# A two-layer perceiver kernel: keys and values projected in other pieces around the transposes, and a weight rounding spread over steps and engines

## The chip, the cores and the metric

One core of one Trainium2 chip. The metric is the device time of one launch in microseconds (us); lower is better. All times of single instructions come from one profiled execution.

## The reference

Two layers, each of a cross attention over 1,024 context positions, a self attention and a gated feed-forward, with a layer norm ahead of each part. Batch 16, 64 latents of width 256, 16 heads of 16. What matters here:

```
x = x + _L0_xattn(ctx, ctx, layernorm(x), mask, ...)   # softmax(q k^T / 4 + mask * -1e9) v, then Wo
x = x + _L0_attn(layernorm(x), ...)
x = x + _L0_ffn(layernorm(x), ...)    # weights rounded to int8 steps: round(w / scale) with scale = max|row| / 127
x = x + _L1_xattn(layernorm(x), ctx, ctx, ...)         # softmax(q k^T / 4) v, then Wo; no mask
x = x + _L1_attn(layernorm(x), ...)
x = x + _L1_ffn(layernorm(x), ...)    # weights and activations rounded to fp4 in blocks of 16
```

## The kernel before

Each engine has its own program, an order written out by hand; semaphores join them. Both cross attentions run as a loop of `STEPS` = 64 steps `s` (16 batches of 4 groups of heads). The first is `first_layer`, the second is in `second_layer`, where the self attention and the start of the feed-forward of finished tiles are woven into the same steps: `tile_at(s, lag)` names the tile whose piece of work stands at step 10 + lag + 8 t.

One step of a cross attention, engine by engine. **TensorE (PE):** `scores` (L801, L807) puts the scores into banks 2 and 3 with queries on partitions and into banks 0 and 1 with keys on partitions; `transposes(s - 1)` (L830) turns the probabilities of the step before, in two halves with a bank each; `project_v(s + 2)` (L755) makes values, one bank, two parts; `turn_column_max` (L814) turns the vector of column maxima; `spread_top` (L821) spreads their overall maximum; `project_k(s + 4)` (L739) makes keys, one bank, two accumulating parts; in even steps `times_v` (L847 to L860, bank "pv") multiplies with the values. **VectorE (DVE):** `column_maxima` (L979; masked L971 and L976), `row_maxima` (L991; masked L988), `tops` (L998), which needs `turn_column_max`, and `below_tops` (L1014 and L1016; masked L1009), which needs `spread_top`. **ScalarE (ACT):** `take_t` (L936), `exponentials` (L919), which needs the row maxima, `take_v` (L909), `take_k` (L882), `column_exponentials` (L927). **GpSimd (POOL):** sums of columns (`spread_rows` L712, `add_columns` L697 to L703), mask conversion, joining of heads. In the second layer `scores(s + 1)` wait for `below_tops(s)` and `exponentials(s)`; in the first for the two maxima of step s alone.

The banks that everything except the scores and the two maxima's transposes uses are a ring of three (5, 6, 7), given out by `Banks.open` in the order in which PE's program opens them. An opening waits until the last holder of that bank has been read out (`taken`), and PE runs in order:

```
        if bank is None:
            bank = self.rotating[self.turn % len(self.rotating)]
            self.turn += 1
        wait(pe, self.taken[bank], self.count[bank])
```

In the second layer only 9 of 16 batches project keys in the loop (steps 4 to 11, 16 to 27, 32 to 43, 56 to 59); the keys of `EarlyKeys.BATCHES` are made earlier and loaded.

The weights of the feed-forwards are made ready inside these loops. `Int8Weights` (first layer; three matrices x, starting at `IW_STEPS` 4, 16, 28) does five steps on DVE: maxima, scale, inverse, rounding of all pieces (L450), subtraction of the rounding constant with conversion to bf16 for all pieces (L457); then three bank units "i" are transposed by PE and taken by ACT. `Fp4Weights` (second layer) does eight DVE steps at `FW_AT`, one on POOL at `FW_SCALE`, and three units "w" at `FW_TRANSPOSE`.

Of the kernel before, what the change touches and what calls it, by code (L numbers as in the profile page):

```python
# [18 lines left out]
ALU = mybir.AluOpType  # L19
# [11 lines left out]
FF = 704  # L31
# [360 lines left out]
class Int8Weights:  # L392
# [3 lines left out]
    STEPS = 5  # L396
# [31 lines left out]
    def step_on_vector(self, dve, x, n):  # L428

        pieces, width = (IC, D) if x < 2 else (KD, FF)  # L430
        first = x * IC
        scale = self.scale[:, first:first + pieces]
        raw = self.raw[:, 0:pieces * width].rearrange("p (c n) -> p c n", n=width)
        whole = self.whole[:, 0:pieces * width].rearrange("p (c n) -> p c n", n=width)
        if n == 0:
            if x == 0:
                dve.wait_ge(self.pad_set, 1)
            dve.wait_ge(self.loaded, (32, 64, 80)[x])
            dve.tensor_reduce(self.mag[:, 0:pieces], raw, AX.X, ALU.max, apply_absolute_value=True)\
                .then_inc(self.step, 1)  # L440
        elif n == 1:
            dve.wait_ge(self.step, 3 * x + 1)
            dve.tensor_scalar(scale, self.mag[:, 0:pieces], 1.0 / QMAX, None, ALU.mult).then_inc(self.step, 1)
        elif n == 2:
            dve.wait_ge(self.step, 3 * x + 2)
            dve.reciprocal(self.inv[:, 0:pieces], scale).then_inc(self.step, 1)
        elif n == 3:
            dve.wait_ge(self.step, 3 * x + 3)
            for c in range(pieces):
                dve.tensor_scalar(raw[:, c, :], raw[:, c, :], self.inv[:, c:c + 1], ROUND, ALU.mult, ALU.add)\  # L450
                    .then_inc(self.rounded, 1)
        else:
            if x >= 1:
                self.banks.wait_filled(dve, ("i", x - 1, self.UNITS - 1))
            for c in range(pieces):
                dve.wait_ge(self.rounded, first + c + 1)
                dve.tensor_scalar(whole[:, c, :], raw[:, c, :], ROUND, None, ALU.subtract).then_inc(self.ready, 1)  # L457
# [119 lines left out]
class CrossAttention:  # L577
# [246 lines left out]
    def transposes(self, pe, s):  # L824

        pe.wait_ge(self.exp_done, s + 1)
        for h in range(2):
            x = self.banks.open(pe, ("t", s, h))
            for n in range(4):
                tr = pe.transpose(self.core.bank[:, x, n * P:(n + 1) * P],  # L830
                                  self.prob[:, s % 2, (4 * h + n) * P:(4 * h + n + 1) * P],
                                  self.core.ident[:, :])
            self.banks.done(tr, ("t", s, h))
# [213 lines left out]
def first_layer(core, ffn_weights, early):  # L1047
# [3 lines left out]
    with ExitStack() as ctx:  # L1051
# [13 lines left out]
        def _(pe):  # L1065
# [15 lines left out]
            for s in range(STEPS + 3):  # L1081
# [9 lines left out]
                if s + 2 < STEPS:  # L1091
                    ca.project_v(pe, s + 2)
                if s < STEPS:
                    ca.turn_column_max(pe, s)
                if s + 4 < STEPS:
                    ca.project_k(pe, s + 4)
                if s < STEPS:
                    ca.spread_top(pe, s)
                for x in range(3):
                    if 6 <= s - IW_STEPS[x] < 9:  # L1100
                        ffn_weights.transposes_on_tensor(pe, x, s - IW_STEPS[x] - 6)
# [37 lines left out]
        def _(pool):  # L1139
# [6 lines left out]
            for s in range(STEPS + 2):  # L1146
# [4 lines left out]
                if s % GROUPS == 2 and s // GROUPS + 1 < B:  # L1151
                    ca.queries(pool, s // GROUPS + 1)
                if s < STEPS:
                    ca.spread_rows(pool, s)
                    ca.add_columns(pool, s)

        @block.scalar
        def _(act):
# [10 lines left out]
            for s in range(STEPS + 1):  # L1169
# [12 lines left out]
                for x in range(3):  # L1182
                    if 6 <= s - IW_STEPS[x] < 9:
                        ffn_weights.take_on_scalar(act, x, s - IW_STEPS[x] - 6)
# [1103 lines left out]
FW_AT = ((2, 3, 4, 5, 6, 7, 8, 9), (17, 19, 21, 22, 25, 27, 29, 30), (37, 38, 41, 43, 45, 46, 49, 51))  # L2288
FW_SCALE = (10, 31, 52)
FW_TRANSPOSE = ((12, 13, 14), (33, 34, 35), (54, 55, 56))  # L2290
# [8 lines left out]
def second_layer(core, weights, old, out, early, given):  # L2299
# [5 lines left out]
    with ExitStack() as ctx:  # L2305
# [15 lines left out]
        def _(pe):  # L2321
# [13 lines left out]
            for s in range(STEPS):  # L2335
                ca.scores(pe, s)
                if s >= 1:
                    ca.transposes(pe, s - 1)
                for t in tile_at(s, 3):
                    sa.latent_transposes(pe, t, norm1.xn_ready)  # L2340
                if s + 2 < STEPS:
                    ca.project_v(pe, s + 2, parts=(0,))
                ca.turn_column_max(pe, s)
                if s + 2 < STEPS:
                    ca.project_v(pe, s + 2, parts=(1,))
                ca.spread_top(pe, s)
                for t in tile_at(s, 8):
                    sa.heads(pe, t)
# [78 lines left out]
        def _(sp):  # L2427
# [3 lines left out]
            for b in range(2, B):  # L2431
# [3 lines left out]
                if b in (5, 10):  # L2435
                    weights.load(sp, b // 5)
# [65 lines left out]
        def _(act):  # L2502
# [10 lines left out]
            for s in range(STEPS):  # L2513
                if s >= 1:
                    ca.take_t(act, s - 1)
                ca.exponentials(act, s)
                for t in tile_at(s, 3):
                    sa.take_latents(act, t)
                for t in tile_at(s, 7):
                    sa.exponentials(act, t)  # L2520
# [4 lines left out]
                if s + 2 < STEPS:  # L2525
                    ca.take_v(act, s + 2)
# [51 lines left out]
        def _(dve):  # L2578
# [22 lines left out]
            for s in range(STEPS):  # L2601
                if s % 2 == 1 and s >= 3:
                    ca.take_pv(dve, (s - 3) // 2)
                ca.column_maxima(dve, s)
                ca.row_maxima(dve, s)
                ca.tops(dve, s)
# [144 lines left out]
```

## Time and profile before

| | us |
|---|---|
| median of 3 runs | 1369.87 (1366.11 to 1375.72) |
| the profiled execution, its own time | 1370.36 |
| its span, first to last instruction | 1368.3 |
| PE busy | 1229.0 (90%) |
| DVE busy | 951.4 (70%) |
| ACT busy | 857.8 (63%) |
| POOL busy | 660.1 (48%) |
| granted PE clock, mean | 0.983 of 2.4 GHz |

A busy PE is not PE at its peak, since matmuls overlap and their ends are modelled; but the engine's order is strict, so a stretch in which PE has nothing to run is lost unless something later absorbs it. The loop of the first layer lies at about 38 to 520 us of the span, that of the second at about 732 to 1253 us.

### The profile page before, as it was taken

The page shows a single profiled execution, that of the slowest core. Times are in us where ns is not written, and L with a number is a line of the kernel's source. Part 1 is how long each engine was busy: PE and PEld are TensorE (multiplying, and loading weights), DVE is VectorE, ACT ScalarE, POOL GpSimd, SP SyncE. Part 2 cuts the span into 40 slices and gives each one's busy share as a digit, 9 for nine tenths or more (in the row PEclk, how much of TensorE's full clock was granted, in tenths as well). Part 3 has the DMA queues.
Part 4 walks back from the last instruction along what each step waited for, and adds up shares of the span by engine and source line. Part 5 has one row for each costly group of instructions (what it writes and reads, how often), then busy time and mean ns, then how long its engine had stood idle before and what let it go on. Part 6 is the DMA issues. An engine that isn't in the chain of part 4 may idle for free. (4 is left out here: it accounts for less than half of the span.)

```text
span 1368.3 us, 32530 instructions
## 1 busy us (share of the span) xinstructions
PE 1229.0 (90%) x12656; PEld 887.8 (65%) x12658; DVE 951.4 (70%) x1543; ACT 857.8 (63%) x1373; POOL 660.1 (48%) x897
## 2 busy tenths in 40 slices
PE   6999999999999988897978999998889998988886
PEld 3666767676777765554645667676667676766654
DVE  3787886787777773684676776676756677756674
ACT  3766767667777754543546667676768676767331
POOL 1665555455565642340013446355654657746533
PEclk9999999999999999999999999999999999999998
DMA  4311322111112203001633021002001132000000
GB/s 157 100 55 55 124 61 77 55 56 55 55 56 85 95 2 115 1 1 31 200 115 88 32 63 54 32 33 63 32 33 54 45 81 64 32 2 2 5 9 19
DMA packets 32853, 78.49 MB, mean 57 GB/s; under 512 B 4416, under 2 KB 16448, under 8 KB 28480
## 3 DMA queue, kind: packets, MB, share of 16 engines
q1 hardware_dynamic: 32704, 76.42, 18.2%
q8 instruction: 103, 1.69, 0.5%
q14 instruction: 46, 0.38, 0.1%
HBM read 69.07 MB, written 7.34 MB: 56 GB/s over the span
## 5 line engine op out<-in xcount | busy, mean ns | idle before, releaser
L697 POOL TENSOR_TENSOR ca_fold<-ca_probT 128x512 f32<-128x512 f32 x128 | 164.0, 1281 | 235.9 <-ACT ca_probT L927 235.4
L936 ACT ACTIVATE ca_probT<-bank 128x512 f32<-128x512 f32 x256 | 140.2, 595 | 110.8 <-PE bank L830 109.5
L801 PE MATMUL bank<-ca_kT,ca_q_blk 32*128 32x512 f32 x512 | 146.4, 648 | 9.7 <-DVE ca_probT L1016 7.1
L830 PE MATMUL bank<-ident,ca_prob 128*128 128x128 f32 x1024 | 144.5, 282 | 11.0 <-DVE ca_picked L1028 5.3
L807 PE MATMUL bank<-ca_q_blk,ca_kT 32*128 32x128 f32 x2048 | 150.9, 286 | 0.0
L927 ACT ACTIVATE ca_probT<-ca_probT 128x1024 f32<-128x1024 f32 x128 | 135.5, 1059 | 18.1 <-DVE ca_probT L1016 12.1
L739 PE MATMUL bank<-ca_ctxT,ca_wk 128*128 128x512 f32 x256 | 123.1, 606 | 9.1 <-DMA ca_bk<-in_L_xattn_bk 9.1
L847 PEld LDWEIGHTS bank<-ca_probT,ca_v 128*32 128x32 f32 x4096 | 109.8, 111 | 32.6 <-issue 26.7
L755 PE MATMUL bank<-wv,ctxT 128*128 128x256 f32 x512 | 129.6, 382 | 1.1 <-ACT fw_upT L383 0.6
L830 PEld LDWEIGHTS bank<-ident,ca_prob 128*128 128x128 f32 x1024 | 109.8, 141 | 31.2 <-DVE ca_picked L1028 7.2
L847 PE MATMUL bank<-ca_probT,ca_v 128*32 128x128 f32 x4096 | 126.9, 276 | 3.3 <-issue 1.8
L755 PE MATMUL bank<-ca_wv,ca_ctxT 128*128 128x256 f32 x512 | 121.8, 381 | 6.8 <-DVE ca_picked L1028 2.3
L807 PEld LDWEIGHTS bank<-ca_q_blk,ca_kT 32*128 32x128 f32 x2048 | 126.2, 188 | 0.3 <-issue 0.3
L1009 DVE TENSOR_TENSOR ca_probT<-ca_masked_col,bank 128x1024 f32<-128x1024 f32 x64 | 78.2, 1223 | 64.3 <-PE bank L821 64.3
L909 ACT ACTIVATE ca_v<-bank 128x512 f32<-128x512 f32 x128 | 76.0, 594 | 54.3 <-PE bank L755 52.4
L979 DVE TENSOR_REDUCE ca_column_max<-bank 128x128 f32<-128x1024 f32 x64 | 78.3, 1223 | 41.9 <-PE bank L807 39.4
L755 PEld LDWEIGHTS bank<-ca_wv,ca_ctxT 128*128 128x128 f32 x512 | 92.4, 190 | 18.8 <-DVE ca_picked L1028 2.7
L712 POOL TENSOR_TENSOR ca_spread_sum<-small,ca_row_sum 128x32 f32<-128x32 f32 x128 | 33.8, 264 | 136.5 <-ACT ca_prob L919 135.5
L919 ACT ACTIVATE ca_prob<-ca_neg_logit,ca_neg_max 128x1024 f32<-128x1024 f32 x64 | 73.5, 1148 | 40.2 <-DVE ca_neg_max L988 40.2
L699 POOL TENSOR_TENSOR ca_fold<-ca_fold 128x256 f32<-128x256 f32 x128 | 93.4, 729 | 10.0
L919 ACT ACTIVATE ca_prob<-bank,ca_neg_max 128x1024 f32<-128x1024 f32 x64 | 71.4, 1115 | 41.9 <-DVE ca_neg_max L991 41.8
L755 PEld LDWEIGHTS bank<-wv,ctxT 128*128 128x128 f32 x512 | 88.0, 191 | 14.8 <-ACT ca_probT L936 2.0
(324 smaller groups left out, 2606.1 us busy)
## 6 DMA issues: line engine op xcount, KB each, us to landing
ca_ctxT<-in_ctxT SPq DMA_DIRECT2D x16, 1024.0 KB, 5.2
ctxT<-in_ctxT SPq DMA_DIRECT2D x16, 1024.0 KB, 4.7
ca_mask_i<-in_mask SPq DMA_DIRECT2D x32, 256.0 KB, 6.3
ek_ctxT<-in_ctxT SPq DMA_DIRECT2D x12, 512.0 KB, 5.6
early_k<-ek_out SPq DMA_DIRECT2D x48, 128.0 KB, 3.5
ca_kT<-early_k SPq DMA_DIRECT2D x12, 512.0 KB, 5.8
ca_mask_col_i<-in_mask_keys SPq DMA_DIRECT2D x16, 256.0 KB, 6.4
lat<-in_x SPq DMA_DIRECT2D x1, 1024.0 KB, 4.9
```

The costliest lines, as they stand in the source:

```text
L697: pool.tensor_tensor(f[:, :, :], p[:, 0:4, :], p[:, 4:8, :], ALU.add).then_inc(self.fold_step, 1)
L699: pool.tensor_tensor(f[:, 0:2, :], f[:, 0:2, :], f[:, 2:4, :], ALU.add).then_inc(self.fold_step, 1)
L739: mm = pe.matmul(self.core.bank[:, self.k_bank, :], self.wk[:, k, m * P:(m + 1) * P], self.ctxT[:, b % 2, k, half * HALF_CTX:(half + 1) * ...
L755: mm = pe.matmul(self.core.bank[:, self.v_bank, r * D:(r + 1) * D], self.ctxT[:, b % 2, k, ch * P:(ch + 1) * P], self.wv[:, k, :], start=( ...
L801: mm = pe.matmul(self.core.bank[:, 2 + half, :], self.q_blk[rows, b % 2, u, :, :], self.kT[rows, b % 2, u, :], start=True, stop=True, tile ...
L807: mm = pe.matmul(self.core.bank[:, half, c * P:(c + 1) * P], self.kT[rows, b % 2, u, c * P:(c + 1) * P], self.q_blk[rows, b % 2, u, :, :], ...
L830: tr = pe.transpose(self.core.bank[:, x, n * P:(n + 1) * P], self.prob[:, s % 2, (4 * h + n) * P:(4 * h + n + 1) * P], self.core.ident[:, :])
L847: pe.matmul(self.core.bank[32 * j:32 * j + 32, x, 0:P], self.v[:, b % 2, ch, m * P + 32 * j:m * P + 32 * j + 32], self.probT[:, n % 2, ch, ...
L919: act.activation(self.prob[:, y, :], source, ACT.Exp, bias=self.neg_max[:, y:y + 1], scale=-1.0 if self.masked else 1.0, accum_out=self.ro ...
L927: act.activation(self.columns(s), self.columns(s), ACT.Exp).then_inc(self.column_exp, 1)
L936: self.banks.free(act.activation(self.probT[:, n % 2, 4 * h:4 * h + 4, 2 * (s % 2) + 1, :], self.core.bank[:, x, :].rearrange("p (n q) -> ...
L979: dve.tensor_reduce(self.column_max[:, y, :], scores.rearrange("p c q -> p q c"), AX.X, ALU.max)\
```

## The change

Four edits.

1. First layer, PE: the first accumulating half of `project_k` stands ahead of `turn_column_max`, the second half behind it.
2. First layer, int8 weights: scale and inverse in one step, then one piece of the rounding for each step (on DVE, 6 pieces or 2), and the subtraction with conversion, piece by piece, by POOL instead of DVE (`whole_on_pool`). The transposes come at 9, 10, 11 steps behind the start instead of 6, 7, 8.
3. Second layer: on PE the first part of the values stands ahead of the transposes, the maxima's transpose between the transposes' halves, the second part behind them, and the self attention's `latent_transposes` behind `spread_top`. On DVE `tops` comes ahead of `row_maxima`. On ACT `take_v` comes ahead of the takes of the tiles' latents and heads, but still behind `exponentials` and behind the tiles' exponentials.
4. Second layer, fp4 weights: other steps (`FW_AT`, `FW_SCALE`, `FW_TRANSPOSE`), and the loads behind batches 6 and 11 instead of 5 and 10.

```
@@ Int8Weights
-    STEPS = 5
+    STEPS = 2 + IC
@@ step_on_vector
         elif n == 1:
             dve.wait_ge(self.step, 3 * x + 1)
             dve.tensor_scalar(scale, self.mag[:, 0:pieces], 1.0 / QMAX, None, ALU.mult).then_inc(self.step, 1)
-        elif n == 2:
             dve.wait_ge(self.step, 3 * x + 2)
             dve.reciprocal(self.inv[:, 0:pieces], scale).then_inc(self.step, 1)
-        elif n == 3:
-            dve.wait_ge(self.step, 3 * x + 3)
-            for c in range(pieces):
-                dve.tensor_scalar(raw[:, c, :], raw[:, c, :], self.inv[:, c:c + 1], ROUND, ALU.mult, ALU.add)\
-                    .then_inc(self.rounded, 1)
-        else:
-            if x >= 1:
-                self.banks.wait_filled(dve, ("i", x - 1, self.UNITS - 1))
-            for c in range(pieces):
-                dve.wait_ge(self.rounded, first + c + 1)
-                dve.tensor_scalar(whole[:, c, :], raw[:, c, :], ROUND, None, ALU.subtract).then_inc(self.ready, 1)
+        elif n - 2 < pieces:
+            c = n - 2
+            if c == 0:
+                dve.wait_ge(self.step, 3 * x + 3)
+            dve.tensor_scalar(raw[:, c, :], raw[:, c, :], self.inv[:, c:c + 1], ROUND, ALU.mult, ALU.add)\
+                .then_inc(self.rounded, 1)
+
+    def whole_on_pool(self, pool, x, c):
+
+        pieces, width = (IC, D) if x < 2 else (KD, FF)
+        if c < pieces:
+            if c == 0 and x >= 1:
+                self.banks.wait_filled(pool, ("i", x - 1, self.UNITS - 1))
+            pool.wait_ge(self.rounded, x * IC + c + 1)
+            pool.tensor_scalar(self.whole[:, c * width:(c + 1) * width], self.raw[:, c * width:(c + 1) * width], ROUND,
+                               None, ALU.subtract).then_inc(self.ready, 1)
@@ CrossAttention
-    def transposes(self, pe, s):
+    def transposes(self, pe, s, halves=range(2)):
-        for h in range(2):
+        for h in halves:
@@ first_layer, PE
+                if s + 4 < STEPS:
+                    ca.project_k(pe, s + 4, parts=(0,))
                 if s < STEPS:
                     ca.turn_column_max(pe, s)
                 if s + 4 < STEPS:
-                    ca.project_k(pe, s + 4)
+                    ca.project_k(pe, s + 4, parts=(1,))
...
-                    if 6 <= s - IW_STEPS[x] < 9:
-                        ffn_weights.transposes_on_tensor(pe, x, s - IW_STEPS[x] - 6)
+                    if 9 <= s - IW_STEPS[x] < 12:
+                        ffn_weights.transposes_on_tensor(pe, x, s - IW_STEPS[x] - 9)
@@ first_layer, POOL (ahead of spread_rows; ACT's take_on_scalar moves by three steps too)
+                for x in range(3):
+                    if 2 <= s - IW_STEPS[x] < ffn_weights.STEPS:
+                        ffn_weights.whole_on_pool(pool, x, s - IW_STEPS[x] - 2)
@@ second layer
-FW_AT = ((2, 3, 4, 5, 6, 7, 8, 9), (17, 19, 21, 22, 25, 27, 29, 30), (37, 38, 41, 43, 45, 46, 49, 51))
-FW_SCALE = (10, 31, 52)
-FW_TRANSPOSE = ((12, 13, 14), (33, 34, 35), (54, 55, 56))
+FW_AT = ((2, 4, 6, 8, 10, 12, 13, 14), (22, 24, 26, 28, 29, 30, 32, 34), (42, 44, 45, 46, 48, 50, 52, 54))
+FW_SCALE = (15, 35, 55)
+FW_TRANSPOSE = ((16, 17, 18), (36, 37, 38), (57, 58, 59))
+FW_LOAD = (6, 11)
@@ second_layer, PE
                 ca.scores(pe, s)
-                if s >= 1:
-                    ca.transposes(pe, s - 1)
-                for t in tile_at(s, 3):
-                    sa.latent_transposes(pe, t, norm1.xn_ready)
                 if s + 2 < STEPS:
                     ca.project_v(pe, s + 2, parts=(0,))
+                if s >= 1:
+                    ca.transposes(pe, s - 1, (0,))
                 ca.turn_column_max(pe, s)
+                if s >= 1:
+                    ca.transposes(pe, s - 1, (1,))
                 if s + 2 < STEPS:
                     ca.project_v(pe, s + 2, parts=(1,))
                 ca.spread_top(pe, s)
+                for t in tile_at(s, 3):
+                    sa.latent_transposes(pe, t, norm1.xn_ready)
@@ second_layer, SP
-                if b in (5, 10):
-                    weights.load(sp, b // 5)
+                if b in FW_LOAD:
+                    weights.load(sp, 1 + FW_LOAD.index(b))
@@ second_layer, ACT
                 ca.exponentials(act, s)
+                for t in tile_at(s, 7):
+                    sa.exponentials(act, t)
+                if s + 2 < STEPS:
+                    ca.take_v(act, s + 2)
                 for t in tile_at(s, 3):
                     sa.take_latents(act, t)
-                for t in tile_at(s, 7):
-                    sa.exponentials(act, t)
                 for t in tile_at(s, 8):
                     sa.take_heads(act, t)
                 for t in tile_at(s, 17):
                     ff.take_latents(act, t)
-                if s + 2 < STEPS:
-                    ca.take_v(act, s + 2)
@@ second_layer, DVE
                 ca.column_maxima(dve, s)
+                ca.tops(dve, s)
                 ca.row_maxima(dve, s)
-                ca.tops(dve, s)
```

## Rows read from the trace of the kernel before

**Rows 1.** Busy time by stretch: the two loops. Length, engines, granted clock, DMA.

```profile
core 0: us, PE busy (x) PEld busy (x) DVE busy (x) ACT busy (x) POOL busy (x), PEclk, DMA share, GB/s
38.00:520.00 482.00, 456.08 (x5058) 332.36 (x5057) 370.38 (x520) 339.23 (x524) 266.50 (x361) 0.99 0.21 64
735.00:1253.00 518.00, 471.12 (x5808) 357.51 (x5807) 360.68 (x552) 357.34 (x566) 288.02 (x448) 1.00 0.14 43
```

**Rows 2.** Waits over the whole span: waiter, releaser, us in total, times, longest.

```profile
PE bank L814 <- DVE ca_column_max L976: 16.2, 28, 3.5
...
PE bank L739 <- ACT ca_v L909: 9.3, 9, 1.3
...
PE bank L755 <- ACT wi_gateT L483: 1.2, 1, 1.2
```

**Rows 3.** First layer, step 16, timeline: start, us, engine, line, [idle before].

```profile
155.18 1.22 DVE L976 TENSOR_REDUCE ca_column_max<-ca_masked_col 128x128 f32<-128x1024 f32 x1
...
156.45 0.33 PE L814 MATMUL bank<-ident,ca_column_max 128*128 128x128 f32 x1 [0.16 <-DVE ca_column_max L976]
...
156.62 1.89 PE L739 MATMUL bank<-ca_ctxT,ca_wk 128*128 128x512 f32 x4
...
158.34 0.27 PE L821 MATMUL bank<-ident,ca_top 128*128 128x128 f32 x1
```

**Rows 4.** Groups by line: int8 pieces on DVE, and a POOL operation like the new.

```profile
L457 DVE TENSOR_SCALAR ca_wi_whole<-ca_wi_raw 128x256 bf16<-128x256 f32 (+1 forms) x14 | 8.0, 632 | 0.0
...
L450 DVE TENSOR_SCALAR ca_wi_raw<-ca_wi_raw,ca_wi_inv 128x256 f32<-128x256 f32 (+1 forms) x14 | 4.4, 380 | 0.0
...
L2228 POOL TENSOR_SCALAR ca_ff_x<-ca_ff_x 128x256 f32<-128x256 f32 x6 | 5.1, 858 | 0.5
```

**Rows 5.** Second layer, odd step 7 up to step 8's scores, timeline.

```profile
781.12 0.70 PE L801 MATMUL bank<-ca_kT,ca_q_blk 32*128 32x512 f32 x2
...
782.46 1.22 DVE L979 TENSOR_REDUCE ca_column_max<-bank 128x128 f32<-128x1024 f32 x1
...
783.60 1.21 DVE L991 TENSOR_REDUCE ca_neg_max<-bank 128x1 f32<-128x1024 f32 x1
...
784.84 1.11 ACT L919 ACTIVATE ca_prob<-bank,ca_neg_max 128x1024 f32<-128x1024 f32 x1 [0.78 <-DVE ca_neg_max L991]
...
785.29 1.88 PE L739 MATMUL bank<-ctxT,ek_wk 128*128 128x512 f32 x4
...
785.88 1.23 DVE L1016 TENSOR_TENSOR ca_probT<-bank,ca_tops_row 128x1024 f32<-128x1024 f32 x1
785.95 0.59 ACT L909 ACTIVATE ca_v<-bank 128x512 f32<-128x512 f32 x1
...
787.36 0.70 PE L801 MATMUL bank<-ca_kT,ca_q_blk 32*128 32x512 f32 x2 [0.20 <-DVE ca_probT L1016]
```

**Rows 6.** PE's timeline: the scores of step 9, behind even step 8.

```profile
795.50 0.70 PE L801 MATMUL bank<-ca_kT,ca_q_blk 32*128 32x512 f32 x2
```

**Rows 7.** PE's timeline, step 34: keys that wait for a value bank.

```profile
1012.57 1.98 PE L739 MATMUL bank<-ctxT,ek_wk 128*128 128x512 f32 x4 [1.28 <-ACT ca_v L909]
```

**Rows 8.** Groups by line on ACT, 735 to 1253 us: table loads, tiles' exponentials.

```profile
L919 ACT ACT_TABLE_LOAD x13 | 16.7, 1283 | 0.2
...
L2042 ACT ACTIVATE ek_out<-ek_out 128x1024 f32<-128x1024 f32 x6 | 6.3, 1045 | 0.0
```

**Rows 9.** Busy time in 4 us from the start of four gaps of PE.

```profile
564.40:568.40 4.00, 2.24 (x6) 1.06 (x6) 2.88 (x5) 1.85 (x4) 1.84 (x2) 1.00 0.00 0
648.60:652.60 4.00, 1.84 (x6) 1.54 (x7) 3.55 (x13) 2.82 (x7) 0.00 (x0) 0.86 0.23 70
711.50:715.50 4.00, 1.99 (x5) 1.06 (x6) 2.14 (x7) 1.76 (x2) 0.96 (x3) 1.00 0.33 88
755.50:759.50 4.00, 2.15 (x22) 1.92 (x22) 1.63 (x3) 2.18 (x4) 1.45 (x2) 0.72 0.02 4
```

**Rows 10.** PE's timeline: scores of steps 4 and 5, second layer.

```profile
757.38 1.22 PE L801 MATMUL bank<-ca_kT,ca_q_blk 32*128 32x512 f32 x2 [1.85 <-DVE ca_probT L1016]
...
766.81 0.70 PE L801 MATMUL bank<-ca_kT,ca_q_blk 32*128 32x512 f32 x2
```

More of the change, by code:

```diff
@@ L433, in step_on_vector @@
         raw = self.raw[:, 0:pieces * width].rearrange("p (c n) -> p c n", n=width)
-        whole = self.whole[:, 0:pieces * width].rearrange("p (c n) -> p c n", n=width)
         if n == 0:
@@ L1182, in _ @@
                 for x in range(3):
-                    if 6 <= s - IW_STEPS[x] < 9:
-                        ffn_weights.take_on_scalar(act, x, s - IW_STEPS[x] - 6)
+                    if 9 <= s - IW_STEPS[x] < 12:
+                        ffn_weights.take_on_scalar(act, x, s - IW_STEPS[x] - 9)
                 if s == Q_STEPS[0]:
```

## The prediction

> **What bounds the kernel now.** I read the busy time by stretch first, then the waits, then one step of each loop in the timeline. In both cross attention loops PE is busy for 456 of 482 us and 471 of 518 us [rows 1]: no other engine comes near, so PE's order sets the pace, and a loop can gain at most the 26 and 47 us in which PE stands. The waits say what those are: 16.2 us at L814 for the column maxima of the first layer, and 9.3 us in nine waits of the second layer's keys (L739) for a value bank that ACT has not read out [rows 2]. The single steps show that DVE is close behind. In the second layer scores start at 781.12 and again at 787.36 [rows 5], a step of 6.24 us; L1016 ends at 787.11, 0.2 us ahead of scores that wait for it. An even step, with `times_v`, takes 787.36 to 795.50, 8.14 us [rows 5, 6].
>
> **First layer, keys in halves.** PE now finishes the values, waits 0.16 us for the turned maxima, runs all of the keys (1.89 us) and spreads the top at 158.34 [rows 3]. With a half (0.94 us) ahead of L814 the wait is filled. The limit is DVE: the column maxima end at 156.40, then L988 and L998 (about 1.25 and 0.28 us) must pass before the spread, so it can't come before about 158.1; gain 0.15 to 0.3 us in a pair of steps, over 29 pairs without other trouble 4 to 9 us. I take 6.
>
> **First layer, int8 by piece.** DVE loses 14 conversions, 8.0 us, and its 14 roundings (4.4 us) are spread over 14 steps instead of coming six at once [rows 4]. The lumps delay L814 today; they are most of the rest of the 16.2 us [rows 2]. Even steps have room behind `times_v`; in odd steps a piece of 0.35 us may show. POOL takes the conversions at about 0.86 us for 256 columns and, scaled, 2.4 for 704 [rows 4]: 12 x 0.86 + 2 x 2.4 = 15 us, hidden behind POOL's idle time (it is busy for 266 of 482 us [rows 1]). Queued behind each are `spread_rows` and `add_columns` of that step; the rounding comes just behind `below_tops`, and the conversion ends about when the column exponentials do, which `add_columns` waits for anyway. If that cover were gone, it costs up to 15 us; if DVE gave back all of its lumps, it gains 9. Against it: a transposed unit "i" takes the bank that the next step's values need, and ACT frees it late; in an odd step that costs 1.2 us [rows 2] (one is named as such; the trace has one per matrix). Units at 9, 10, 11 behind even starts lie twice in odd steps instead of once: 3 x 1.2 = 3.6 us back. Net I take -2. First layer together: -8 us, between -15 and +5.
>
> **Second layer, who holds the bank.** This decides. The ring has three banks. Before, a step opens transposes, transposes, values, and then keys: the fourth opening gets the bank of the first, half 0 of the transposes, read out long ago. After, it opens values, transposes, transposes, and whatever PE does first behind `spread_top` gets the *values'* bank: the keys, or the tile's pieces ("sx", "so", "fx", "ss", "sb", "sy"), or "pv". I wrote the openings of all 64 steps out in both orders: in 59 of them (all except 0, 1, 3, 62, 63) the first opening behind the spread now follows the values. It must wait for `take_v(s + 2)`, which ACT does behind `exponentials(s)`, and those wait for the row maxima, which DVE now does after `tops`. That this wait is real is seen today in a step in which the tile's heads shift the ring: the keys stand 1.28 us for L909 [rows 7].
>
> **Its price.** Counted from the start of the scores, in a step of now 6.24 us [rows 5]: column maxima 1.34 to 2.56; L814 at 2.6, ready for `tops` at about 3.0; `tops` 0.28; row maxima 1.21, to 4.45; exponentials start 4.5 (3.72 now); `take_v` begins 1.11 later, at 5.6, and takes 0.59: bank free at 6.2. PE has spread the top and starts keys at 4.17 now; it would start them at 6.23. That is 2.06 us in each of 59 steps: +121.5 us. The chain of DVE itself does not change: row maxima cover the wait for the spread, L1016 still ends at about 6.0, and it no longer matters, since scores come at 8.3. The bound from below: even at today's time of `take_v`, 5.42 [rows 5], keys would start 1.3 us later, 59 x 1.3 = 77 us.
>
> **What is already there.** PE's idle time in this loop, 47 us [rows 1], is partly at the same place (the 9.3 us of rows 2 above all) or comes from DVE being late from the step before, which a longer step gives back. Going through PE's timeline by step, 20 us lie between the spread and the next scores in the 59 steps, and 15 us are turned maxima later than 2.9 us into the step: -35, at most -42, at least -25.
>
> **What ACT adds.** In 6 steps the tiles' exponentials (1.045 us) stand ahead of `take_v`: +6. Behind each of 13 square roots the table for the exponentials is loaded again, 1.28 us [rows 8]; it starts when `take_t` is done, now about 3.8 us into the step since its second half comes behind L814, so exponentials start at 5.1 or so instead of 4.5: 12 x 0.7 = +8. Sum +14, from 0 to 20.
>
> **fp4 steps and loads.** DVE's steps move, and the loads wait for units transposed at steps 18 and 38, ahead of first use at 22 and 42, so that SP holds no context load back that is due. In steps that PE's wait makes longer DVE has 2 us to spare: 0.
>
> **The clock.** Each such step has a PE gap of about 1.9 us. After a gap of 1.85 us PE ran at the lower of its levels, 1.2 GHz instead of 2.4: the scores took 1.22 instead of 0.70 us, and the step 757.38 to 766.81 took 9.43 instead of 8.14 [rows 6, 10]: 1.29 us. Of four gaps of 1.7 to 2.2 us two were followed by that (granted 0.86 and 0.72) and two were not (1.00) [rows 9]. So I take half of 59: +38 us, bounds 0 and 76. The Trainium skill has a rule here that speaks against the change (TensorE: Matmul & The Clock Gate, "A second HAM failure mode: psum-queue depth-cycling"): a PE that cycles through banks and idles shortly and often can see its clock go back and forth. By it all 59 would count, the upper bound; the trace agrees for half of the gaps. Another page (Perfetto Trace Analysis, "Matmul Optimizations") asks to use all eight banks; the ring of three is what makes this wait, and the sum does not need that page.
>
> **Sum.** -8 + 121.5 - 35 + 14 + 38 = +131. On the profiled execution's own 1370.4 (span 1368.3 and 2.1 around it), 0.5 above the median of the runs shown, this is 1501 us.
>
> **Rivals.** (1) The same wait with the clock staying up: +93, 1463 us. For it: with 2 of 4 us idle from 711.50 on the clock stayed at its upper level [rows 9]. (2) The clock falls in nearly each step: +169, 1539 us. For it: the gaps come in every step. (3) The wait is only 1.3 us, because the exponentials start as early as now (if DVE's turned maxima came without delay), and the clock stays: -8 + 77 - 35 + 5 = +39, 1409 us. (4) The other side, faster: the values' bank is free before the spread is done, so that nothing waits and the reordering only fills gaps: -8 in the first layer, and in the second the wait for L821 covered, at most 0.2 us in 28 steps without keys in the loop, -6: 1356 us. It decides if `take_v` ends before 4.2 us into the step; today it ends at 5.42 with an earlier row maximum [rows 5], so almost nothing speaks for it. (5) The int8 and key edits do nothing and the second layer's wait is hidden by luck of other waits: 1370 us.
>
> **How the numbers follow.** Forecast 1501: 0.50. Rival 1: 0.21. Rival 2: 0.13. Rival 3: 0.08. Rival 4: 0.04. Rival 5: 0.04. Forecast, 1 and 2 with their bounds make 1440 to 1550, which leaves out the other three and some of the upper tail. A measurement of this kernel tells changes of about 1% from none. Slower by over 1%: 0.92; within 1%: 0.04; faster: 0.04.
>
> **What the changed profile would show.** If right: in the waits, PE L739, L847 and tile lines waiting for ACT ca_v L909 some 59 times, in total 90 to 130 us, not 9.3; odd key steps of 8.2 us and even ones of 10.2 instead of 6.24 and 8.14; PE idle over 120 us in the second loop; granted clock there below 1.00, about 0.9; the first loop some 8 us shorter, L814's 16.2 us mostly gone, L457 gone from DVE, and its successor on POOL near 0.86 us. If no row waits for L909, the ring argument is wrong, and so is the sign. If the wait is there and the time is 1463, only the clock was wrong.

## The result, and the profile after

The changed kernel takes 1539.47 us (median of four runs, 1534.36 to 1544.93), the kernel before 1369.56 beside it: ratio 1.124, 95% interval 1.118 to 1.129. The direction was right and the time lies inside the range, but 38 us above the forecast of 1501. The profiled execution has a span of 1539.5 us against 1368.3, so 171.2 us are to be found. From the first scores to the last scores of each loop, the first layer takes 472.1 us instead of 480.9, the second 698.7 instead of 516.7; what lies outside the loops is 2.0 us shorter. -8.8 + 182.0 - 2.0 is the whole difference.

Busy time by stretch of the changed kernel, its first and second loop (columns as in [rows 1]):

```profile
core 0: us, PE busy (x) PEld busy (x) DVE busy (x) ACT busy (x) POOL busy (x), PEclk, DMA share, GB/s
38.00:511.00 473.00, 449.25 (x5055) 337.52 (x5055) 367.38 (x506) 338.50 (x523) 279.40 (x376) 0.99 0.22 66
725.00:1421.00 696.00, 538.99 (x5777) 400.01 (x5778) 361.18 (x547) 359.37 (x561) 284.69 (x443) 0.89 0.11 32
```

The second line already splits the loss. DVE, ACT and POOL work as long as before, to within 4 us: no work was added. PE stands for 157.0 us (696.00 - 538.99) where it stood for 46.9, and it is busy for 539.0 us with the same matmuls that took 471.1, at a granted clock of 0.89. So of the 178 us between the two stretches 110 are waiting and 68 are the same matmuls run more slowly; from scores to scores, 182 us, it is 111 and 71.

Whom PE waits for, over the whole span (waiter, releaser, us in total, times, longest; L742 is the keys, L2018, L1967, L1936, L1995 and L2158 are pieces of the tiles, L850 is `times_v`, L912 is `take_v`, formerly L909):

```profile
PE bank L742 <- ACT ca_v L912: 42.7, 20, 2.8
PE bank L2018 <- ACT ca_v L912: 23.0, 6, 4.1
PE bank L850 <- ACT ca_v L912: 16.5, 7, 4.1
PE bank L1967 <- issue: 15.8, 6, 2.8
PE bank L1936 <- ACT ca_v L912: 13.9, 7, 2.0
PE bank L1995 <- ACT ca_v L912: 12.6, 6, 2.1
PE bank L2158 <- ACT ca_v L912: 9.9, 5, 2.0
...
PE bank L817 <- DVE ca_column_max L979: 6.7, 4, 2.6
```

With two smaller rows these are 53 waits for `take_v` and 123.5 us, where [rows 2] had nine of the keys and 9.3 (one more, of `times_v`, took 1.4). The six at L1967, which the profile puts down to "issue" (nothing that it can name), are waits for `take_v` too: the one of step 15 ends at 869.81, just behind `take_v` at 869.71, and with row maxima first (below) the profile names `take_v` for one of them. That makes 59 waits and 139.3 us. The last row is the first layer's wait for the column maxima, 16.2 us in 28 waits before.

Timeline of step 7, the step of [rows 5] (start, us, engine, line, idle before):

```profile
780.65 0.70 PE L804 MATMUL bank<-ca_kT,ca_q_blk 32*128 32x512 f32 x2
...
783.70 0.29 DVE L1001 TENSOR_REDUCE ca_top<-bank 128x1 f32<-128x128 f32 x1 [0.49 <-PE bank L817]
783.90 1.21 DVE L994 TENSOR_REDUCE ca_neg_max<-bank 128x1 f32<-128x1024 f32 x1
...
784.73 0.27 PE L824 MATMUL bank<-ident,ca_top 128*128 128x128 f32 x1
...
785.15 1.11 ACT L922 ACTIVATE ca_prob<-bank,ca_neg_max 128x1024 f32<-128x1024 f32 x1 [0.49 <-DVE ca_neg_max L994]
...
786.26 0.59 ACT L912 ACTIVATE ca_v<-bank 128x512 f32<-128x512 f32 x1
...
786.90 1.98 PE L742 MATMUL bank<-ctxT,ek_wk 128*128 128x512 f32 x4 [1.90 <-ACT ca_v L912]
...
788.81 0.70 PE L804 MATMUL bank<-ca_kT,ca_q_blk 32*128 32x512 f32 x2
```

Read it from the bottom: scores at 788.81 follow keys, keys waited 1.90 us for the value bank, the bank was read out behind the exponentials, those waited for the row maxima. `tops` now stands ahead of them. The spread has been done since 785.0. The step takes 8.16 us instead of 6.24.

PE's timeline one step on, keys of step 8 with what follows:

```profile
795.15 3.65 PE L742 MATMUL bank<-ctxT,ek_wk 128*128 128x512 f32 x4 [1.99 <-ACT ca_v L912]
798.73 1.95 PE L850 MATMUL bank<-ca_probT,ca_v 128*32 128x128 f32 x64
800.83 0.70 PE L804 MATMUL bank<-ca_kT,ca_q_blk 32*128 32x512 f32 x2
```

The same gap, but here the clock fell behind it: the four key matmuls last 3.65 us instead of 1.98. This step takes 12.02 us, before it was 8.14; without a fall (from 2.4 to 1.2 GHz), even key steps take 10.26. In the second loop PE ran at 1.2 GHz for 153.6 us, 36 falls that touch 42 of 63 steps, where before there was one, of 3.4 us.

### The profile page after: what moved, and what is told of

The parts are those of the page before. It is cut to its first block and busy times, and to the rows that moved or that the text cites. A ratio compares the mean times of both kernels' runs of the same rounds, so it can differ in the third digit from the quotient of the medians.

```text
span 1539.5 us, 32595 instructions
## 1 busy us (share of the span) xinstructions
PE 1291.4 (84%) x12658; PEld 936.8 (61%) x12658; DVE 952.5 (62%) x1529; ACT 863.2 (56%) x1373; POOL 672.1 (44%) x911
## 3 DMA queue, kind: packets, MB, share of 16 engines
q1 hardware_dynamic: 32704, 76.42, 16.2%
## 5 line engine op out<-in xcount | busy, mean ns | idle before, releaser
L804 PE MATMUL bank<-ca_kT,ca_q_blk 32*128 32x512 f32 x512 | 154.1, 679 | 7.9 <-DVE ca_probT L1019 5.5
L810 PE MATMUL bank<-ca_q_blk,ca_kT 32*128 32x128 f32 x2048 | 158.0, 295 | 0.0
L833 PE MATMUL bank<-ident,ca_prob 128*128 128x128 f32 x1024 | 151.5, 281 | 4.9 <-DVE ca_picked L1031 2.6
L850 PE MATMUL bank<-ca_probT,ca_v 128*32 128x128 f32 x4096 | 134.9, 287 | 23.4 <-ACT ca_v L912 16.5
L850 PEld LDWEIGHTS bank<-ca_probT,ca_v 128*32 128x32 f32 x4096 | 117.7, 116 | 51.3 <-issue 43.5
L758 PE MATMUL bank<-wv,ctxT 128*128 128x256 f32 x512 | 142.2, 402 | 0.4 <-DVE ca_q L958 0.3
L742 PE MATMUL bank<-ca_ctxT,ca_wk 128*128 128x512 f32 x256 | 129.1, 603 | 9.2 <-DMA ca_bk<-in_L_xattn_bk 9.2
L742 PE MATMUL bank<-ctxT,ek_wk 128*128 128x512 f32 x160 | 98.2, 749 | 44.7 <-ACT ca_v L912 42.7
L810 PEld LDWEIGHTS bank<-ca_q_blk,ca_kT 32*128 32x128 f32 x2048 | 132.8, 198 | 0.0
L833 PEld LDWEIGHTS bank<-ident,ca_prob 128*128 128x128 f32 x1024 | 117.9, 143 | 24.2 <-issue 7.4
L885 ACT ACTIVATE ca_kT<-bank,ek_bk 64x512 f32<-64x512 f32 x80 | 54.6, 682 | 105.3 <-PE bank L742 104.7
L912 ACT ACTIVATE ca_v<-bank 128x512 f32<-128x512 f32 x128 | 75.8, 592 | 52.8 <-PE bank L758 52.7
```

The costliest lines, as they stand in the source:

```text
L742: mm = pe.matmul(self.core.bank[:, self.k_bank, :], self.wk[:, k, m * P:(m + 1) * P], self.ctxT[:, b % 2, k, half * HALF_CTX:(half + 1) * ...
L758: mm = pe.matmul(self.core.bank[:, self.v_bank, r * D:(r + 1) * D], self.ctxT[:, b % 2, k, ch * P:(ch + 1) * P], self.wv[:, k, :], start=( ...
L804: mm = pe.matmul(self.core.bank[:, 2 + half, :], self.q_blk[rows, b % 2, u, :, :], self.kT[rows, b % 2, u, :], start=True, stop=True, tile ...
L810: mm = pe.matmul(self.core.bank[:, half, c * P:(c + 1) * P], self.kT[rows, b % 2, u, c * P:(c + 1) * P], self.q_blk[rows, b % 2, u, :, :], ...
L833: tr = pe.transpose(self.core.bank[:, x, n * P:(n + 1) * P], self.prob[:, s % 2, (4 * h + n) * P:(4 * h + n + 1) * P], self.core.ident[:, :])
L850: pe.matmul(self.core.bank[32 * j:32 * j + 32, x, 0:P], self.v[:, b % 2, ch, m * P + 32 * j:m * P + 32 * j + 32], self.probT[:, n % 2, ch, ...
```

## The experiments

**Each layer alone.** The change is put into one layer, the other keeps the old code; first the first layer, then the second:

> The changed first layer with the second layer as before. My theory (all of the loss is in the second layer, the first loop gained 8.8 us of its own): 1361 us, between 1357 and 1366, and the first loop 472 us as in the changed kernel. Rival (the first layer's edits are what slows, by the port or POOL's 15 us): 1370 or more.

> The first layer as before, the second changed. My theory: 1548 us, between 1535 and 1560, that is the changed kernel plus the 9 us that the first layer gained. Rival (the two layers' edits act on each other, by the clock or the loads): clearly outside of that.

Measured: 1360.16 us, ratio 0.993 (0.991 to 0.995), and 1549.08 us, ratio 1.131 (1.128 to 1.133). Loops: 471.8 and 516.2 us with the first layer changed, 478.5 and 698.7 with the second. The two parts add up to the whole; all of the loss is in the second.

**Who holds the bank.** One line in the second layer's PE order skips one bank of the ring behind the transposes, so that the keys get another bank than the values'. Nothing else of the new order is touched:

```diff
                     ca.transposes(pe, s - 1, (1,))
+                banks.turn += 1
                 if s + 2 < STEPS:
```

> The changed kernel with one line more in PE's order of the second layer: behind the second half of the transposes the ring is turned on by one, so that the first opening behind the spread gets the bank of the transposes' first half instead of the values'. All orders of all engines stay as changed. My theory (who holds the bank is the whole loss): no waits for take_v, clock back at 1.00 in the loop, 1362 us, between 1350 and 1385. Rival (the later row maxima, exponentials and take_v cost by themselves): 1420 us or more.

Measured: 1376.81 us, ratio 1.005 (1.003 to 1.007). Timeline of step 7 (PE and ACT) and the second loop by stretch:

```profile
780.57 1.88 PE L742 MATMUL bank<-ctxT,ek_wk 128*128 128x512 f32 x4
...
781.99 0.59 ACT L912 ACTIVATE ca_v<-bank 128x512 f32<-128x512 f32 x1
```

```profile
725.00:1257.00 532.00, 472.93 (x5782) 361.28 (x5785) 361.42 (x547) 357.33 (x561) 286.72 (x443) 0.99 0.14 42
```

Keys start 1.4 us before `take_v` and wait for nothing. Key steps are back at 6.27 and 8.10 us, PE is busy for 472.9 us, and the clock falls only four times, for 13.7 us. `take_v` itself is no earlier in its step: the exponentials still wait for the late row maxima. So neither the reordered DVE nor the split values cost much by themselves; the bank does. One line takes back 163 of the 170 us.

The loop of 534.7 us is still 17.9 longer than the old one. It lies in steps with tile work (17, 23, 39, 49 and 57 by 2.2 to 2.5 us each, 13, 45, 53 and 61 by 1.3 to 1.9); the fp4 edit is about 3 of it (below). The waits name a part of the rest:

```profile
PE bank L817 <- DVE ca_column_max L982: 13.9, 22, 1.3
PE bank L742 <- ACT ca_v L912: 11.9, 11, 1.2
```

PE now comes to the second layer's turned maxima before they are ready (before, 5.0 us in 8 waits), and beside tile work the keys still wait for `take_v`. How much of the 17.9 us each makes was not settled. What it does say: with nearly all of the wait gone, the new order gives the second layer nothing.

**The row maxima.** DVE's order alone is put back:

```diff
                 ca.column_maxima(dve, s)
-                ca.tops(dve, s)
                 ca.row_maxima(dve, s)
+                ca.tops(dve, s)
```

> The changed kernel, with DVE's row maxima ahead of the tops again in the second layer, nothing else. Exponentials then start 0.75 us earlier in a step and so does take_v. My theory: odd key steps 7.4 us instead of 8.16, gaps of 1.2 us instead of 1.9, 59 x 0.75 = 44 us less from the wait, and of the clock's share (about 70 us) most goes too, since the gaps are shorter: 1430 us, between 1410 and 1500. Rival (DVE's order is not on the path): 1540, as changed.

Measured: 1483.79 us, ratio 1.083 (1.080 to 1.085); step 7 (ACT and PE), then the loop:

```profile
779.28 1.11 ACT L922 ACTIVATE ca_prob<-bank,ca_neg_max 128x1024 f32<-128x1024 f32 x1
...
781.01 1.98 PE L742 MATMUL bank<-ctxT,ek_wk 128*128 128x512 f32 x4 [1.29 <-ACT ca_v L912]
```

```profile
725.00:1362.00 637.00, 506.58 (x5776) 380.29 (x5778) 356.64 (x546) 356.19 (x562) 286.89 (x444) 0.94 0.12 35
```

The gap falls from 1.90 to 1.29 us, an odd key step from 8.16 to 7.56, as expected. The centre of 1430 was missed on both counts. From scores to scores PE stands 27 us less, not 44, since the long gaps behind table loads (4.07 us, below) stay. And PE's busy time falls by 32 of the 71 us, since the clock still fell 19 times, for 81.9 us: 15 times behind the 18 gaps of 2.2 to 4.1 us, three times behind the some 40 gaps of about 1.3 us. Of the wait of 1.9 us in step 7 a third is the maxima's order; the rest stays as long as the ring gives the keys that bank.

**The values taken first.** ACT reads the values out ahead of the exponentials:

```diff
+                if s + 2 < STEPS:
+                    ca.take_v(act, s + 2)
                 ca.exponentials(act, s)
...
-                if s + 2 < STEPS:
-                    ca.take_v(act, s + 2)
```

> The changed kernel, with take_v ahead of the exponentials on ACT in the second layer; the ring stays as changed. The values are ready on PE at about 4.2 us into a step, so their bank is free at about 4.8 instead of 6.2, and the exponentials start at 4.8 instead of 4.5. My theory: keys start at 4.85, odd key steps 6.8 us, no clock falls; 59 x 0.7 = 41 less the 35 that was idle anyway, less 9 from the first layer: 1375 us, between 1365 and 1400. Rival (the exponentials are the path, not the bank): 1540 or slower.

Measured: 1399.97 us, ratio 1.020 (1.018 to 1.021). Step 7:

```profile
782.51 0.60 ACT L912 ACTIVATE ca_v<-bank 128x512 f32<-128x512 f32 x1 [0.33 <-PE bank L758]
783.01 1.11 ACT L922 ACTIVATE ca_prob<-bank,ca_neg_max 128x1024 f32<-128x1024 f32 x1
783.16 1.98 PE L742 MATMUL bank<-ctxT,ek_wk 128*128 128x512 f32 x4 [0.64 <-ACT ca_v L912]
```

ACT now waits for PE to have filled the bank, and PE for ACT to have read it: 0.64 us are left, and an odd step takes 6.91. PE ran at 1.2 GHz for only 10.2 us in the loop. The time is at the upper end of what I had given, 25 us above its centre: among others the scores now wait for the later exponentials, 9.2 us in eight waits. The same opening that costs 1.9 us behind the exponentials costs 0.6 ahead of them, which shows that the wait is the place of `take_v` in ACT's queue.

**The clock by itself.** Useless matmuls (128x256, into a bank that was read out) fill PE's gap behind the spread, so that the wait stays and PE doesn't stand. First six of them, then three:

```diff
                 ca.spread_top(pe, s)
+                if 2 <= s < STEPS - 2:
+                    banks.wait_taken(pe, ("t", s - 1, 0))
+                    for n in range(6):
+                        pe.matmul(bank_of[:, banks.at[("t", s - 1, 0)][0], 0:D], ca.wv[:, 0, 0:P], ca.wq[:, 0, :],
+                                  start=True, stop=True)
```

> The changed kernel, with six matmuls of 128x256 (about 1.4 us) of no use behind each spread of the steps 2 to 61 of the second layer, into the bank of the transposes' first half, once it has been read. They lie in the gap in which PE waits for take_v, and their results are never read. My theory (the gap makes the clock fall, and that is about 70 of the 182 us that the loop lost): the clock stays at 1.00 in the loop, the steps keep 8.16 and about 10.0 us, 1475 us, between 1455 and 1500. Rival (the clock has another cause, or its price is small): 1535 us or more, since work was added.

> The changed kernel with three matmuls of no use in each gap instead of six. Six took 2.76 us, more than the gap of 1.9, and made an undisturbed odd step 8.60 instead of 8.16 us. Three take 1.35 us and fit. My theory (the gap makes the clock fall): clock at 1.00 in the loop, steps of 8.16, loop 638 us instead of 699 as changed and 656 with six: 1480 us, between 1472 and 1490. Rival (the rest of 0.55 us of gap is enough for the clock to fall, or the first filled kernel was faster by another cause): 1500 or more.

Measured: 1499.24 us with six, ratio 1.093 (1.091 to 1.094), and 1488.48 with three, 1.085 (1.082 to 1.088). PE in step 7, with three, and the second loops, with six and with three:

```profile
780.13 1.46 PE L2360 MATMUL bank<-wq,wv 128*128 128x256 f32 x6
...
782.19 1.98 PE L742 MATMUL bank<-ctxT,ek_wk 128*128 128x512 f32 x4 [0.60 <-ACT ca_v L912]
```

```profile
723.00:1377.00 654.00, 620.79 (x6492) 491.94 (x6492) 362.78 (x547) 358.86 (x561) 287.75 (x443) 1.00 0.11 34
```

```profile
723.00:1367.00 644.00, 561.12 (x6138) 427.10 (x6138) 361.45 (x546) 359.25 (x561) 286.69 (x443) 0.98 0.12 35
```

Six took 2.76 us, twice what I had reckoned, since each makes two rows on PE; they overfill the gap, and an odd step takes 8.60 us. Still the clock is 1.00 and the kernel 40 us faster than the changed one. Three leave the undisturbed step at 8.17, and of the 21 steps that no fall touches in either kernel 20 are as long as in the changed one, to 0.01 us: so here only the clock differs. The loop takes 646.6 us instead of 698.7, with six falls left (23.9 us at 1.2 GHz instead of 153.6). That is 52.1 us for 129.7 us at 1.2 GHz; at this rate the six falls left cost some 10, and without them the loop would take some 637. With the clock up the loss would be some 120 us, and the clock's share of it is about 62.

**The fp4 steps alone.** The old kernel with the change's steps and loads for the fp4 matrices:

```diff
+FW_AT = ((2, 4, 6, 8, 10, 12, 13, 14), (22, 24, 26, 28, 29, 30, 32, 34), (42, 44, 45, 46, 48, 50, 52, 54))
+FW_SCALE = (15, 35, 55)
+FW_TRANSPOSE = ((16, 17, 18), (36, 37, 38), (57, 58, 59))
+FW_LOAD = (6, 11)
```

> The kernel before with the fp4 weights' steps and loads of the changed one, nothing else. My theory of the prediction (this edit costs nothing): within 4 us of the kernel before. Rival (the 15 us that remain with the ring turned on by one are from here): 1380 us or more.

Measured: 1372.93 us, ratio 1.001 (1.000 to 1.002), second loop 519.9 us. Nothing that counts, as predicted.

**The first layer's two edits.** First the keys in halves alone, on the old kernel:

```diff
+                if s + 4 < STEPS:
+                    ca.project_k(pe, s + 4, parts=(0,))
...
-                    ca.project_k(pe, s + 4)
+                    ca.project_k(pe, s + 4, parts=(1,))
```

> The kernel before with the keys in halves around the column maxima's transpose in the first layer, nothing else. My theory: odd to even steps gain 0.16 us each, and the lumps of the int8 steps are covered for 0.9 us each: 6 to 10 us less, 1362 us. Rival (the gain of the first loop is that of the int8 steps): 1367 to 1370.

Measured: 1359.86 us, ratio 0.992 (0.990 to 0.994); first loop 470.7 us, L814's wait is down to:

```profile
PE bank L814 <- DVE ca_column_max L976: 7.5, 6, 2.6
```

That is the whole gain of the first layer: the int8 edits as made give nothing on top. Then they are kept, with the old second layer, but the units are transposed behind even steps only:

```diff
+UNIT_STEPS = (8, 10, 12)
...
-                    if 9 <= s - IW_STEPS[x] < 12:
+                    if s - IW_STEPS[x] in UNIT_STEPS:
```

> The second layer as before; the changed first layer, but with the int8 transposes 8, 10 and 12 steps behind their start (even steps all) instead of 9, 10, 11. In the changed kernel the steps behind the odd ones (14, 16, 26, 38, 40) are 1.2 to 1.6 us longer, because the values wait for the unit's bank. My theory: 6 x 1.4 = 8 us less than the changed first layer with the second as before: 1353 us, between 1348 and 1358. Rival (the wait moves with the units to the even steps): 1360.

Measured: 1352.33 us, ratio 0.985 (0.984 to 0.987), first loop 463.8 us. PE's values in step 14, behind the unit of step 13, in the changed kernel and here:

```profile
136.45 1.97 PE L758 MATMUL bank<-ca_wv,ca_ctxT 128*128 128x256 f32 x8 [1.20 <-ACT wi_gateT L486]
```

```profile
134.92 1.91 PE L758 MATMUL bank<-ca_wv,ca_ctxT 128*128 128x256 f32 x8
```

The wait for the unit's bank is gone: 1.20 us here. The changed kernel has two of these waits for each of three matrices, the kernel before had one; without the six the loop is 8.0 us shorter (471.8 to 463.8) and, with DVE's relief, 6.9 shorter than with the key halves alone.

**A version faster than both.** The last one, with only the second layer's ACT order taken from the change, `take_v` ahead of the tile's latents:

```diff
                 ca.exponentials(act, s)
-                for t in tile_at(s, 3):
-                    sa.take_latents(act, t)
                 for t in tile_at(s, 7):
                     sa.exponentials(act, t)
+                if s + 2 < STEPS:
+                    ca.take_v(act, s + 2)
+                for t in tile_at(s, 3):
+                    sa.take_latents(act, t)
```

> The even-units kernel with one more edit in the second layer: ACT's order of the change alone (take_v ahead of the takes of the tiles' latents and heads), PE's and DVE's orders as before. My theory: in the 7 steps in which the tiles' heads stand ahead of the keys, PE's wait for take_v shrinks from 1.28 to about 0.6 us: 4 to 8 us less than the even units alone, 1346 us. Rival (the wait passes to the take of the heads): 1352.

Measured: 1344.00 us, ratio 0.980 (0.978 to 0.982), the fastest of the study, 8.3 us below the even units alone; 6.3 of them lie in the second loop, the other 2 in code that is the same. Its wait for L912 at the keys, nine waits and 9.3 us in [rows 2]:

```profile
PE bank L742 <- ACT ca_v L912: 2.1, 5, 0.5
```

Steps 18, 26, 42 and 58 go from 12.4 to 11.08 us, 34 and 50 by 1.0 and 0.9; steps 13, 45, 53 and 61, where the tiles' latents now come later, lose 0.5 each.

## Why the prediction was right, and where it was 38 us short

The largest term, the ring's bank, was right in mechanism and near in size, and it decided the sign and most of the loss; the 38 us come from two terms that were too small, ACT's additions and the clock, and the second hangs on the first. The second loop's 182.0 us in the parts of my sum, from the records of PE step by step. Behind the spread PE stands 141 us in the 59 steps, where it stood 20: 113 are the wait (59 x 1.92), 28 what some steps have above it. Ahead of the spread it stands 8.3 us instead of 18.6. The rest, 71 us, is PE being busy for longer.

| part of the sum | predicted | measured |
|---|---|---|
| wait for the ring's bank, 59 steps | +121.5 | +113 |
| ACT's additions to it | +14 | +28 |
| already there | -35 | -30 (20 behind, 10 ahead of the spread) |
| clock | +38 | +71 |
| second loop | +138.5 | +182 |

**The wait: right.** Keys were to start 6.23 us into an odd step, and in step 7 they start at 6.25. The step grew by 1.92 and not 2.06, because scores no longer wait for L1016, the 0.2 us that [rows 5] showed. The steps were called at 8.2 and 10.2 (8.16 in step 7; step 22, undisturbed, 10.26), the waits for `take_v` at some 59, 90 to 130 us (59, and 139.3 us with ACT's additions). The skipped bank proves the cause: 6.27 and 8.10 us without it.

**The clock: right mechanism, half its size.** "So I take half of 59: +38 us." For gaps of the length that I had counted on, the half held: behind the 41 waits of 1.4 to 2.3 us the clock fell 20 times. Behind the 18 of 2.8 to 4.1 us, which ACT's work made longer, it fell 15 times, and eight of the nine falls that last twice as long as the others stand there. (The 36th is in step 4, where the kernel before has its one.) By their time at 1.2 GHz, 72 and 79 us, the short gaps have about 33 of the 71 us, near my 38, and the long ones about 36. I had priced all 59 as gaps of 1.9 us. A fall also cost more where it hit: the keys take 3.65 instead of 1.98 us (step 8 above), while the fall of [rows 10] put the turned maxima back by 1.5 us and the step won 0.2 of that back. The loop loses less than 71, about 62 us by the three filling matmuls: slower matmuls cover some 9 us of standing. The Trainium skill (TensorE: Matmul & The Clock Gate, "A second HAM failure mode: psum-queue depth-cycling") tells of a clock that goes back and forth because PE idles briefly and often, and the trace agrees with its 36 falls; the page gives no share, and that all 59 would count was my reading of it: 35 did.

**ACT: half of it missed.** "Sum +14, from 0 to 20." The tiles' exponentials came out at +0.9 us in five of six steps, +1.6 in the last, +6 together as predicted. The table loads were mis-sized: I costed 0.7 us for a load ahead of the exponentials, which I let start when `take_t` is done, 3.8 us into the step. ACT and PE in step 12 of the changed kernel, scores at 831.16:

```profile
831.35 1.38 ACT L885 ACTIVATE ca_kT<-bank,ek_bk 64x512 f32<-64x512 f32 x2 [2.16 <-PE bank L742]
832.75 1.06 ACT L930 ACTIVATE ca_probT<-ca_probT 128x1024 f32<-128x1024 f32 x1
833.83 1.28 ACT L1862 ACT_TABLE_LOAD   x1
835.12 0.20 ACT L1862 ACTIVATE ca_sn_std<-ca_sn_var 128x1 f32<-128x1 f32 x1
835.35 1.08 ACT L939 ACTIVATE ca_probT<-bank 128x512 f32<-128x512 f32 x2
836.45 1.28 ACT L922 ACT_TABLE_LOAD   x1
837.75 1.11 ACT L922 ACTIVATE ca_prob<-bank,ca_neg_max 128x1024 f32<-128x1024 f32 x1
838.85 0.59 ACT L912 ACTIVATE ca_v<-bank 128x512 f32<-128x512 f32 x1
839.59 3.58 PE L850 MATMUL bank<-ca_probT,ca_v 128*32 128x128 f32 x64 [4.07 <-ACT ca_v L912]
```

Two tables are loaded ahead of `take_v`, the root's and the exponentials', and `take_t` stands between them. Exponentials start 6.59 us into the step and the values' bank is free at 8.28, so PE's gap is 4.07 us, 2.1 more than in other even steps. The kernel before has the same order and nearly the same times; its step 12, scores at 818.15:

```profile
820.55 1.28 ACT L1854 ACT_TABLE_LOAD   x1
...
822.08 1.08 ACT L936 ACTIVATE ca_probT<-bank 128x512 f32<-128x512 f32 x2
823.18 1.28 ACT L919 ACT_TABLE_LOAD   x1
824.48 1.11 ACT L919 ACTIVATE ca_prob<-bank,ca_neg_max 128x1024 f32<-128x1024 f32 x1
...
825.58 0.59 ACT L909 ACTIVATE ca_v<-bank 128x512 f32<-128x512 f32 x1
```

There exponentials start at 6.33 and `take_v` ends at 8.02, and it cost nothing, since no opening of that step waited for the values' bank. So this could be read before the change: I had taken the second load and left out the root's, ahead of `take_t`. Six steps (12, 20, 28, 36, 44, 60) have both, 13 us where I had 4; there `take_v` ends 8.0 to 8.3 us into the step in the kernel before and 8.3 to 8.4 in the changed one. Steps 23, 31, 39, 47 and 55 have 0.8 more than others, 4 us, as I had costed. The other 5 us are scattered. No run moved the table loads alone, so their price is read from the timeline and not tested.

**Already there: near.** The 20 us behind the spread went as predicted; of the 15 ahead of it, 10. Some turned maxima stay late: in steps 16 and 56 they come at 4.4 to 4.5 us, since the tile's scores on PE stand behind the wait too and DVE needs them first, and in 19, 27, 35, 43, 51 and 59 at 3.65 (3.88 before), since DVE does a finished tile's sum and its norm (L1040, L1854) ahead of the column maxima, which start 2.4 us into step 19.

**First layer: total right, parts not.** Predicted -8, measured -8.8. Keys in halves brought 8 to 10 us alone (470.7 us; the old first loop takes 478.5 to 481.2 in three traces), at the upper end of the 4 to 9 that I gave or above it: a pair of undisturbed steps went from 14.25 to 13.95, the 0.3 of my upper end, and steps in which DVE is late gain more. The int8 edits on top came to about nothing, predicted -2: the changed first loop takes 470.2 to 472.1 us in seven traces. Even units took out all six waits for 8.0 us, of which the three new ones are about half: near the 3.6 that I had. DVE's relief then gave back only 3, not 5.6. POOL's conversions cost what was said (14.2 us, predicted 15), hidden:

```profile
L459 POOL TENSOR_SCALAR ca_wi_whole<-ca_wi_raw 128x256 bf16<-128x256 f32 (+1 forms) x14 | 14.2, 1011 | 32.7 <-DVE ca_wi_raw L449 32.5
```

**Rivals.** The measured time is the one of rival 2, but not for its reason: the clock fell behind 35 of the 59 waits, not nearly all, and the rest is ACT's. Rival 1 (clock up) is what three filling matmuls come near: 1488, not 1463, for ACT's additions and six remaining falls. Rival 3 (wait of 1.3 us) is the kernel with row maxima first: 1484, not 1409, for the clock, and because its long gaps behind the table loads stay. Rivals 4 and 5 fell with the first row of the waits.

## What to carry to other kernels

Where buffers go round in a ring, the order of openings decides who waits for whom: before you move one, write out whose buffer each opening inherits and how deep in the other engine's queue its reader stands. A gap that comes in each step has to be priced twice, as a wait and in matmuls at 1.2 GHz, and the second is seen by filling the gap with useless work. When a wait passes to another reader, price it by where that reader stands in each kind of step and not in the plainest one: here `take_v` was 2.1 us later in six steps, in the kernel before as in the changed one, and both the wait and the clock's share grew by it.

## What was unexpected of the hardware

Whether PE's clock falls went with the length of the gap, by shares and not by one limit: behind waits of 1.4 to 2.3 us it fell 20 of 41 times, behind those of 2.8 to 4.1 us 15 of 18 times; with row maxima first three times behind some 40 gaps of about 1.3 us and 15 times behind 18 of 2.2 to 4.1; with gaps of 0.6 us in undisturbed steps it ran at 1.2 GHz for 10.2 us. In the other direction, adding work to PE made the kernel faster: six useless matmuls in each step, 1539 to 1499 us, three of them 1488. A matmul of 128x128 by 128x256 in fp32 makes two rows, 0.24 us each (three of them the six rows of 1.46 us above).
